# Grouped feed-forward and the layer norm behind it in one stage

## The reference, cut to what matters

```python
xg = xn.reshape(8, m, 128)                                  # eight groups of 1024 tokens
h1 = jnp.einsum('gmh,goh->gmo', xg, W1) + b1[:, None, :]    # 128 -> 512
h2 = jnp.einsum('gmo,gho->gmh', h1, W2) + b2[:, None, :]    # 512 -> 128, no nonlinearity between
x = x + s * silu(h2)
xn = (x - mean(x)) / sqrt(var(x) + 1e-5)                    # over the 128 channels of each token
```

## Time and profile before

| | |
|---|---|
| median of 3 runs | 2907.16 us (2902.68 to 2909.36) |
| profiled execution | 2906.29 us, its span 2904.5 us |
| busy share of the span | PE 92%, DVE 74%, ACT 67%, POOL 38% |
| grouped feed-forward stage | 1229.83 to 1275.52 us |
| norm stage behind it | 1275.52 to 1315.68 us |
| mean granted TensorE clock | 0.956 |

### The profile page before, as it was taken

One profiled execution on the slowest core, in us unless ns is written; L12 is line 12 of the kernel. 1 busy time (PEld: TensorE's weight loads), 2 busy tenths in 40 slices (PEclk: granted clock), 3 DMA queues, 4 the chain that ended last, 5 costly groups with the idle time before them and its releaser, 6 DMA issues. The chain is left out here.

```text
span 2904.5 us, 62166 instructions
## 1 busy us (share of the span) xinstructions
PE 2675.6 (92%) x21644; PEld 1785.4 (61%) x21644; DVE 2159.2 (74%) x3766; ACT 1934.7 (67%) x5521; POOL 1101.1 (38%) x1260
## 2 busy tenths in 40 slices
PE   7799999997889979888879999998998999999898
PEld 4577897774554434345547777776444777777644
DVE  4577565776675669856769999997447999999676
ACT  4366665666764544344369999997437999999744
POOL 0233343331004543310045555554215555555431
PEclk9699998998999989989989999999998999999999
DMA  4200121000000000030000000000000000000000
GB/s 147 77 23 21 52 68 30 22 22 12 9 17 0 1 0 1 10 74 9 20 9 2 2 2 2 2 2 10 12 1 10 2 2 2 2 2 2 2 22 37
DMA packets 83170, 53.92 MB, mean 19 GB/s; under 512 B 28848, under 2 KB 75568, under 8 KB 82864
## 3 DMA queue, kind: packets, MB, share of 16 engines
q1 hardware_dynamic: 78768, 41.56, 5.1%
q0 software_dynamic: 4096, 8.40, 1.0%
HBM read 31.59 MB, written 18.35 MB: 17 GB/s over the span
## 5 line engine op out<-in xcount | busy, mean ns | idle before, releaser
L2124 ACT ACTIVATE probs<-banks,minus_max,rnorm 128x128 f32<-128x128 f32 x1024 | 460.0, 469 | 4.3 <-DVE minus_max L2220 4.3
L1996 PE MATMUL banks<-weights,hf 128*128 128x512 f32 x768 | 431.1, 645 | 24.4 <-POOL hf L336 13.5
L2039 POOL TENSOR_TENSOR qk_cross<-qk_raw,rope_scaled 128x512 f32<-128x512 f32 x256 | 325.9, 1274 | 25.5 <-ACT qk_raw L2157 11.5
L2049 POOL TENSOR_TENSOR qk_rot<-qk_rot,rnorm 128x512 f32<-128x512 f32 x128 | 133.5, 1043 | 291.8 <-DVE qk_rot L2253 283.3
L2124 ACT ACTIVATION_READ_ACCUMULATOR probs<-banks,minus_max,rnorm 128x1 f32 x1024 | 222.6, 217 | 0.0
L712 ACT ACTIVATE probs<-banks,minus_max 128x128 f32<-128x128 f32 (+1 forms) x512 | 207.9, 425 | 13.1 <-DVE minus_max L751 13.1
L2200 DVE COPY probs_t<-banks 128x512 f32<-128x512 f32 x256 | 175.9, 687 | 54.5 <-PE banks L1974 53.9
L1974 PEld LDWEIGHTS banks<-ident,probs 128*128 128x128 f32 x1024 | 126.8, 140 | 134.4 <-issue 134.4
L2246 DVE TENSOR_TENSOR qk_rot<-qk_raw,rope_scaled 128x512 f32<-128x512 f32 x256 | 175.8, 727 | 0.0
L2234 DVE TENSOR_REDUCE sumsq<-qk_sq 128x16 f32<-128x1024 f32 x128 | 154.8, 1209 | 26.9 <-issue 19.9
L2005 PE MATMUL banks<-ident,qk_rot 128*128 128x128 f32 x1024 | 159.6, 279 | 10.0 <-DVE qk_rot L2253 4.9
(11 more groups left out here) (354 smaller groups left out, 6985.2 us busy)
## 6 DMA issues: line engine op xcount, KB each, us to landing
sorted_x<-zero_rows SPq DMA_DIRECT2D x10, 512.0 KB, 6.0
rows_in<-sorted_x SPq DMA_DIRECT2D x18, 256.0 KB, 3.1
sorted_y<-rows_out SPq DMA_DIRECT2D x18, 256.0 KB, 2.4
x_res<-in_x SPq DMA_DIRECT2D x8, 512.0 KB, 6.7
out_x<-x_res SPq DMA_DIRECT2D x16, 256.0 KB, 2.0
w1b<-in_L_ffn_w SPq DMA_DIRECT2D x8, 256.0 KB, 3.9
s_branch<-in_L_ffn_w SPq DMA_DIRECT2D x8, 256.0 KB, 5.8
w1g<-in_L_ffn_W SPq DMA_DIRECT2D x8, 256.0 KB, 3.0
```

The source lines that it names most:

```text
L1996: pe.matmul(ps[:, misc(k, j)], hf[:, n // 2 % 2, 0, n % 2 * P:(n % 2 + 1) * P], wqkv[:, w:w + QW], start=True, stop=True).then_inc(*S[name ...
L2039: return pool.tensor_tensor(by_half(tw[:, n, at]), by_half(qk[:, n, at])[:, :, ::-1, :], tab[:, n, 2 * w + 1].rearrange("p (a d) -> p a d" ...
L2124: last = act.activation(pr[:, k % 2, head], ps[:, 2 * (k % 2) + par, c * P:(c + 1) * P], ACT.Exp, scale=rn[:, k % 4, head:head + 1], bias= ...
```

## The change

The two stages become one over 16 chunks (`R`), in which each engine's loop works on several chunks at a time. In pass c TensorE folds the next group's weights (odd c), multiplies chunk c+1, turns chunk c-2 to rows and turns chunk c-5 back. ScalarE applies Silu to chunk c, scales chunk c-4 and copies chunk c-6 out to `xn`. VectorE makes the shift of chunk c-4, the product of chunk c-1, takes a fold over, adds chunk c-1 to `x`, and takes the moments of chunk c-3. GpSimd takes the power of each chunk; the clearing, now in seven parts, stands four parts before the first power and one before each of the next three. SP loads the weights of seven groups, waits for the clearing, and loads twelve of the convolution's pieces, the eighth group's weights and the other pieces. The separate call of `layer_norm` is gone, and with it one stage boundary. The moments come from bn_stats on rows; before, they came from matmuls.

```diff
-        grouped_ffn(nc, ps, m, a)
...
-            layer_norm(nc, ps, m, m["x"], m["xn"], ahead=conv_pairs, clear=clear)
+            grouped_ffn(nc, ps, m, a, conv_pairs, clear)
...
+    S, R, W = STEPS, 2 * ROUNDS, 4
+    PREP_AT, FFN_AT, IN_AT, BACK_AT = 0, 2, 4, 6
+    EARLY = 4
...
+                for g in range(GROUPS - 1):
+                    weights(g)
+                sp.wait_ge(S["g5"].sem, S["g5"].base + len(clear))
+                for dst, src in ahead[:12]:
+                    sp.dma_start(dst, src).then_inc(S["loaded"].sem, 16)
+                weights(GROUPS - 1)
+                for dst, src in ahead[12:]:
...
+                fold(0)
+                for c in range(-1, R + 5):
+                    if c >= 0 and c % 2 == 1 and c // 2 + 1 < GROUPS:
+                        fold(c // 2 + 1)
+                    if c + 1 < R:
+                        pe.wait_ge(*S["v1"].at(0, (c + 1) // 2))
+                        pe.wait_ge(*S["silu"].at(0, c - 1))
+                        pe.matmul(ps[:, FFN_AT + (c + 1) % 2], wc[:, (c + 1) // 2 % 2], m["xn"][:, tokens(c + 1)], start=True,
+                                  stop=True).then_inc(*S["m2"].inc)
+                    if 0 <= c - 2 < R:
+                        n = c - 2
+                        pe.wait_ge(*S["added"].at(0, n))
+                        pe.wait_ge(*S["scaled"].at(0, n - 2))
...
+                    if 0 <= c - 5 < R:
+                        n = c - 5
+                        pe.wait_ge(*S["scaled"].at(0, n))
+                        pe.wait_ge(*S["normed"].at(0, n - 2))
...
+                folded(0)
+                for c in range(R + 5):
+                    if 0 <= c - 4 < R:
+                        n = c - 4
+                        dve.wait_ge(*S["deviation"].at(0, n))
+                        dve.scalar_tensor_tensor(shift[:, n], mv[:, n, :, 0], -1.0, rs[:, n], ALU.mult, ALU.mult)\
+                            .then_inc(*S["centered"].inc)
+                    if 0 <= c - 1 < R:
+                        n = c - 1
+                        dve.wait_ge(*S["silu"].at(0, n))
+                        dve.tensor_tensor(gate[:, n % 2], gate[:, n % 2], m["s"][:, tokens(n)], ALU.mult)\
+                            .then_inc(*S["weighed"].inc)
+                    if c >= 0 and c % 2 == 1 and c // 2 + 1 < GROUPS:
+                        folded(c // 2 + 1)
+                    if 0 <= c - 1 < R:
+                        dve.wait_ge(*S["weighed"].at(0, c - 1))
+                        dve.tensor_tensor(m["x"][:, tokens(c - 1)], m["x"][:, tokens(c - 1)], gate[:, (c - 1) % 2], ALU.add)\
+                            .then_inc(*S["added"].inc)
+                    if 0 <= c - 3 < R:
+                        n = c - 3
+                        dve.wait_ge(*S["mean"].at(0, n))
+                        for t in range(W):
+                            last = dve.bn_stats(st[:, n % 2, t], ps[:, IN_AT + n % 2, t * P:(t + 1) * P])
...
+                        dve.wait_ge(*S["variance"].at(0, n))
+                        dve.tensor_scalar(rs[:, n], mv[:, n, :, 1], EPS, None, ALU.add).then_inc(*S["m3"].inc)
...
+                for n in range(R):
+                    for part in clear[:EARLY] if n == 0 else clear[n + EARLY - 1:n + EARLY]:
+                        pool.memset(part, 0.0).then_inc(S["g5"].sem, 1)
+                    pool.wait_ge(*S["m3"].at(0, n))
+                    pool.tensor_tensor(rs[:, n], rs[:, n], m["half"][:, 0:W], ALU.pow).then_inc(*S["deviation"].inc)
...
-    return (head, rest, bi, bt, bo, win, wout), pairs, [head, rest[:, 0:BLK], rest[:, BLK:]]
+    return (head, rest, bi, bt, bo, win, wout), pairs, [head] + [rest[:, k:k + 9] for k in range(0, 2 * BLK - HEAD, 9)]
```

More of the change, by code:

```diff
@@ L1651, in _, with grouped_ffn, tokens @@
                 out(R - 1)
-def grouped_ffn(nc, ps, m, a):
-    S = STEPS
-    R = GROUPS // 2
+def grouped_ffn(nc, ps, m, a, ahead, clear):
+    S, R, W = STEPS, 2 * ROUNDS, 4
     IT = INTER // P
+    PREP_AT, FFN_AT, IN_AT, BACK_AT = 0, 2, 4, 6
+    EARLY = 4
     with ExitStack() as mem:
         buf = on_chip(nc, mem)
[L1663 to L1667, removed]
+        w1, w2, b1 = buf("w1g", P, 2, IT, P), buf("w2g", P, 2, IT, P), buf("b1g", P, 2, IT)
+        b2, wc, bc = buf("b2g", P, 2), buf("wc", P, 2, P), buf("bc", P, 2)
+        gate, rows = buf("gate", P, 2, C), buf("ln_rows", P, 2, W, P)
+        st, mv = buf("ln_stats", P, 2, W, 6), buf("ln_moments", P, R, W, 2)
+        rs, shift = buf("ln_scale", P, R, W), buf("ln_shift", P, R, W)
+        def tokens(c):
+            return slice(c * C, (c + 1) * C)
+        with Stage(1, fetched0=2 * GROUPS, fetched1=2 * GROUPS, m1=GROUPS, v1=GROUPS, m2=R, silu=R, weighed=R, added=R, mean=R,
+                   squared=R, variance=R, m3=R, deviation=R, centered=R, scaled=R, copied=R, normed=R), nc.Block() as block:
@@ L1668, in _, with weights @@
             @block.sync
             def _(sp):
[L1670 to L1681, removed]
+                def weights(g):
+                    u = g % 2
+                    sp.wait_ge(*S["v1"].at(0, g - 2))
+                    sp.wait_ge(S["first"].sem, PRIME)
+                    for dst, src in ((w1[:, u], a["L2_ffn_W1"][g].rearrange("(c p) h -> p c h", p=P)),
+                                     (w2[:, u], a["L2_ffn_W2"][g:g + 1].rearrange("g (c p) h -> p (g c) h", p=P)),
+                                     (b1[:, u], a["L2_ffn_b1"][:, g * IT:(g + 1) * IT]),
+                                     (b2[:, u:u + 1], a["L2_ffn_b2"][g:g + 1].rearrange("g p -> p g"))):
+                        sp.dma_start(dst, src).then_inc(*S[f"fetched{u}"].inc)
@@ new lines, in _ @@
+                for g in range(GROUPS - 1):
[5 more added lines that the diff above has]
+                for dst, src in ahead[12:]:
+                    sp.dma_start(dst, src).then_inc(S["loaded"].sem, 16)
+                sp.wait_ge(S["loaded"].sem, S["loaded"].base + 16 * len(ahead))
@@ L1683, in _, with fold @@
             @block.tensor
             def _(pe):
[L1685 to L1701, removed]
+                def fold(g):
+                    u = g % 2
+                    pe.wait_ge(*S[f"fetched{u}"].at(0, 4 * (g // 2) + 3))
+                    pe.wait_ge(*S["v1"].at(0, g - 2))
+                    for c in range(IT):
+                        pe.matmul(ps[:, PREP_AT + u, 0:P], w1[:, u, c], w2[:, u, c], start=(c == 0), stop=(c == IT - 1))
+                    for c in range(IT):
+                        mm = pe.matmul(ps[:, PREP_AT + u, P:P + 1], w2[:, u, c], b1[:, u, c:c + 1], start=(c == 0),
+                                       stop=(c == IT - 1))
+                    mm.then_inc(*S["m1"].inc)
@@ new lines, in _ @@
+                fold(0)
[12 more added lines that the diff above has]
+                        for t in range(W):
+                            mm = pe.transpose(ps[:, IN_AT + n % 2, t * P:(t + 1) * P],
+                                              m["x"][:, n * C + t * P:n * C + (t + 1) * P], m["ident"][:])
+                        mm.then_inc(*S["mean"].inc)
+                    if 0 <= c - 5 < R:
+                        n = c - 5
+                        pe.wait_ge(*S["scaled"].at(0, n))
+                        pe.wait_ge(*S["normed"].at(0, n - 2))
+                        for t in range(W):
+                            mm = pe.transpose(ps[:, BACK_AT + n % 2, t * P:(t + 1) * P], rows[:, n % 2, t], m["ident"][:])
+                        mm.then_inc(*S["copied"].inc)
@@ L1705, in _ @@
                 act.preload_act_table_set("silu_and_others")
[L1706 to L1711, removed]
+                for c in range(R + 6):
+                    if c < R:
+                        act.wait_ge(*S["m2"].at(0, c))
+                        act.wait_ge(*S["added"].at(0, c - 2))
+                        act.activation(gate[:, c % 2], ps[:, FFN_AT + c % 2], ACT.Silu,
+                                       bias=bc[:, c // 2 % 2:c // 2 % 2 + 1]).then_inc(*S["silu"].inc)
+                    if 0 <= c - 4 < R:
+                        n = c - 4
+                        act.wait_ge(*S["centered"].at(0, n))
+                        act.wait_ge(*S["copied"].at(0, n - 2))
+                        for t in range(W):
+                            last = act.activation(rows[:, n % 2, t], ps[:, IN_AT + n % 2, t * P:(t + 1) * P], ACT.Identity,
+                                                  scale=rs[:, n, t:t + 1], bias=shift[:, n, t:t + 1])
+                        last.then_inc(*S["scaled"].inc)
+                    if 0 <= c - 6 < R:
+                        n = c - 6
+                        act.wait_ge(*S["copied"].at(0, n))
+                        act.activation(m["xn"][:, tokens(n)], ps[:, BACK_AT + n % 2], ACT.Copy).then_inc(*S["normed"].inc)
@@ L1713, in _, with folded @@
             @block.vector
             def _(dve):
[L1715 to L1727, removed]
+                def folded(g):
+                    u = g % 2
```

(25 more changed lines are left out.)

## The result

The changed kernel takes 2910.0 us (median of 20 runs, 2906.61 to 2915.18) against 2904.84 us for the kernel before, run beside it (20 runs, 2901.52 to 2912.47). The ratio is 1.0017 [1.001, 1.0024]: slower by 5.2 us. That is just inside the 0.2% that the prediction calls "no difference", with an interval wholly above 1. The forecast was +6.6 us, about 2914, in the range of 2903 to 2925. The likeliest case there, 2910 to 2919, is met at its lower edge; by the bounds given there the result counts as "no change" (chance 0.40) and not as "slower" (0.51).

What follows compares the result with a forecast made beforehand. VectorE, waiting for GpSimd's power, was taken to set the round: 25.2 + 58 + 5.5 + 3.8 = 92.5 us against 85.85, +6.6 on the median of 2907.16, about 2914; range 2903 to 2925.

Steps and rivals of the forecast that it cites:

- likeliest case: Whole kernel: TensorE's clock is mixed in the merged stage, 2910 to 2919 us; chance 45%.
- no change: Whole kernel: a difference under 0.2%, 5.8 us, giving 2901.3 to 2913.0 us; chance 0.40.
- What sets the round: VectorE's loop: each shift waits about 1.2 us for GpSimd's uncovered power, making a round 4.1 us at full clock.
- head: Stage start to first shift: 22.7 us at full clock to 28.0 at half, taken as 25.2.
- drain: Stage end, after the last shift: 3.5 us as in the integer stage's norm, plus 0.29 to the next stage; 3.8.
- The mixed clock: 13 rounds: TensorE's clock changes to and fro, 58 us between 54.8 at full and 66.6 at half clock.
- Its signs of being wrong: Merged stage: shifts under 3.5 us apart, or VectorE idle for TensorE or a DMA instead of GpSimd.
- rival (a): Merged stage: TensorE at half clock throughout, +14 to +18 us, 2921 to 2925; chance 20%.
- upper bound of 103.9: Merged stage wholly at half clock: 28.0 + 66.6 + 9.3 = 103.9 us, +18; four transposes take 0.85 us.
- rival d: SP's loads: the weights of group 7 come late, 2920 us or more; chance 2%.
- rival (c): Rounds: power already done when VectorE asks, TensorE's 3.05 us rules, stage 74.2, -12 us, 2895; chance 10%.
- (b): Merged stage: full clock from the second fold on, +1 to +3 us, 2908 to 2910; chance 23%.

Runs made afterwards that it cites:

- the idle time filled: Changed kernel with four extra 256-column matmuls in each even pass, result unread; ratio 1.0002 against the kernel before.
- The covered kernel: Changed kernel with VectorE's shift moved behind the product and the add, which then run beside GpSimd's power; ratio 1.0003 against the kernel before.
- both edits: Changed kernel with VectorE's shift behind product and add, and folds made and taken over one pass earlier; 2895.5 us, ratio 0.9969 against the kernel before.

## Why the prediction was right, point by point

**What sets the round.** Right. It named the order on VectorE, with a wait of 1.19 us and a round of 4.1; measured 1.12 to 1.16 in all 16 shifts, and 4.03. Without the power a round is 2.94, with two powers 5.0.

**The sum.** 91.35 us against 92.5: head 23.3 (25.2), 13 rounds 58.13 (58), last two 5.60 (5.5), drain 4.32 (3.8). The head came out near its lower bound of 22.7, since the clock rose early, in the second fold: it was granted at 0.50 up to 1238, at 1.00 from 1239.

```profile
1230.03 2.07 PE L1703 MATMUL banks<-w2g,w1g 128*128 128x128 f32 x8 [6.17 <-DMA b2g<-in_L_ffn_b]
1231.89 1.71 PE L1705 MATMUL banks<-b1g,w2g 128*128 128x1 f32 x8
...
1237.62 1.70 PE L1703 MATMUL banks<-w2g,w1g 128*128 128x128 f32 x8
1239.16 0.95 PE L1705 MATMUL banks<-b1g,w2g 128*128 128x1 f32 x8
```

In TensorE's timeline above the bias matmuls of the first fold take 1.71 us, those of the second 0.95. The drain was mis-sized by 0.5: in the stage that it was taken from the earlier trace rows the transposes back follow the scaling at once, and here they wait 0.63 us, until ScalarE has copied an earlier chunk out. The stage's excess is thus 5.5 instead of 6.6; most of the rest of the 4 us between 2910.0 and 2914 is the median it was added to, 2907.16 of 3 runs, which is 2904.84 over 20.

**The mixed clock.** Right in kind: 0.77 in the rounds, and folds of 1.84 and 3.18 us side by side. The prediction added 3.2 us for it to 54.8. With the idle time filled the rounds take 53.10, so their work was put 1.7 too high (a plain round is 4.03 for 4.1, and a fold that isn't waited for adds 0.13 for 0.3), and the low clock, at 5.0 us, 1.8 too low. That 58 meets 58.13 is luck: the two errors cancel. In the 13 rounds the low clock costs only where a fold is waited for: those without a fold take 4.03 to 4.05 us at any granted clock from 0.50 to 1.00, those with one 4.16 to 5.93. That the clock would change to and fro because TensorE idles at full clock and is full at half was the author's estimate: with the idle time filled the rounds' clock was 0.94 instead of 0.77, but what makes it change no run shows.

**Its signs of being wrong.** Two of them showed in part. VectorE idled for TensorE too, 4.65 us in the 13 rounds beside 14.6 for GpSimd; and three of the five folds there were waited for over 1 us, which was to speak for rival (a), half clock throughout. It was half clock in some rounds only: by the cuts above 1.00 in the first and 0.50 in that with the longest wait.

**The clock over transposes.** The four transposes at 1268.72 take 0.44 us to the fold behind them, at a granted clock of 1.00, not 0.85 as in the earlier trace rows, at 0.50; and the stage came to 91.35 us, not to the upper bound of 103.9. Transposes are 26.2 of TensorE's 62.67 busy us in this stage. It mixes matmuls in and so can't tell whether transposes alone would have raised the clock; in the earlier trace rows, where nothing but transposes ran, it rose to 0.91.

**The free parts.** Clearing, loading order and late weights (rival d) cost nothing, as said: all clearing first changed nothing, and TensorE waited for a DMA only at the first fold.

**What failed: the price in rival (c).** The forecast itself didn't rest on it. It said that with the power met already done, the round would be about 2.9 and TensorE's 3.05 would rule, 74.2 us for the stage. The covered kernel shows the premise true and the price wrong: 85.55 us. The step compared each engine's work in a round as if the engines were free of each other. TensorE's transposes wait for ScalarE's scaling of two chunks before, the fold is queued behind them, and VectorE's add behind the fold, a ring of 5.50 us that no engine's busy time shows. Only with the fold moved too does the stage come near that price, 75.64. Rivals (a) and (b), one clock throughout, did not occur.

## What to carry to other kernels

When several engines run one loop over staggered chunks, follow the rings through the in-order queues (which wait stands ahead of which instruction on each engine) and not only the busy time of a round: the slowest ring sets it, and taking one away shows the next (here the power's, 4.03 us a round, then the fold's, 5.50 in a round with a fold). A tiny operation on another engine whose result is asked for first thing in the next pass costs its whole round trip in every pass (here 1.12 us of 4.03); put independent work between the two, and ask for anything that several queues must pass a pass early. Two edits that each regain only the loss (5.8 and 5.3 us of the stage here) can be worth nearly three times that together (15.7).

## What the runs showed of the hardware

GpSimd's power of 128x4 takes 1.01 to 1.04 us each of 16 times in the changed kernel, where VectorE waits for it. With both edits it takes 1.33 to 1.40 in nine of 16. Two of the 16, with VectorE's product beside each:

```profile
1268.43 1.01 POOL L1802 TENSOR_TENSOR ln_scale<-ln_scale,minus_half 128x4 f32<-128x4 f32 x1 [1.70 <-DVE ln_scale L1792]
1268.59 0.68 DVE L1770 TENSOR_TENSOR gate<-gate,s_branch 128x512 f32<-128x512 f32 x1
...
1271.40 0.68 DVE L1770 TENSOR_TENSOR gate<-gate,s_branch 128x512 f32<-128x512 f32 x1
1271.57 1.38 POOL L1802 TENSOR_TENSOR ln_scale<-ln_scale,minus_half 128x4 f32<-128x4 f32 x1 [2.13 <-DVE ln_scale L1792]
```

In all nine slow cases the product was running when the power began, and the power ended 0.86 to 0.90 us after the product's end. In four others the product began 0.08 to 0.29 us after the power, and neither took longer: 1.01 and 0.68 us. In the last three nothing of the kind ran beside the power.

So where the product was first, the power lost 0.32 to 0.39 us; where the power was first, neither lost anything. Why the power takes longer beside the product no run here tested.

Additional matmuls whose result nobody reads made this stage 5.4 us shorter (85.90 for 91.35); the edit changed nothing else, and the granted clock rose from 0.72 to 0.86.
